# Histogram of the destinations moved into the first layer, attention terms in two parts, and the scatter ahead of the attention's gathers

## What is computed

```python
x = x + segment_sum(layernorm(x)[src] * w[:, None], dst) @ W.T + b      # 200,000 edges, dst sorted
y = layernorm(x)                                                       # layer 2
h = (y @ W_gat).reshape(M, 4, 4)                                       # 4 heads x 4 experts
a_src, a_dst = (h * att_src).sum(-1), (h * att_dst).sum(-1)
e = leaky_relu(a_src[src2] + a_dst[dst2], 0.2)                         # 131,072 edges, unsorted, + self loops
alpha = softmax of e over the edges of each dst2
scores = layernorm(segment_sum(h[src2] * alpha) + b_gat) ... .mean(heads)
out = x + sum over the 2 best experts of gate * (gelu(y @ W1[e] + b1[e]) @ W2[e] + b2[e])
```

## Time and profile before

| | |
|---|---|
| median of 3 runs | 4101.27 us (4099.21 to 4102.57) |
| the profiled execution, its own time | 4099.11 us |
| span of its trace, first to last instruction | 4097.2 us |
| mean granted TensorE clock | 0.859 |
| busy: PE, DVE, ACT, POOL | 3044.6, 1891.6, 743.4, 2766.0 us |
| block B, first instruction to barrier | 109.5 to 2066.2 |
| block of attention terms | 2066.2 to 2079.2 |
| block C | 2079.2 to 3536.3 |

### The profile page before, as it was taken

How to read it: one execution, slowest core, us unless ns; L and a number is a source line. 1 busy time by engine, 2 the same in 40 slices (tenths; PEclk the granted TensorE clock), 3 DMA queues, 4 the chain that set the end, 5 groups by cost and what they waited for, 6 DMA issues and landing times. The chain is left out here.

```text
span 4097.2 us, 58613 instructions
## 1 busy us (share of the span) xinstructions
PE 3044.6 (74%) x13541; PEld 2398.9 (59%) x13542; DVE 1891.6 (46%) x4731; ACT 743.4 (18%) x2065; POOL 2766.0 (68%) x2845
## 2 busy tenths in 40 slices
PE   1666666777878887988879999999999500266946
PEld 0444444555656665666668888888888500154734
DVE  7633444454545565444334444343431000397749
ACT  6200000001111111222222222222222100031411
POOL 6577777777777777777657777777777777301850
PEclk6877878788888998999989999999999855587978
DMA  9433333334444444444322222222222210004839
GB/s 346 144 107 105 109 112 111 114 115 115 119 117 121 119 121 121 127 127 130 112 80 64 61 64 59 63 61 64 61 64 62 44 18 4 31 23 168 305 143 363
DMA packets 298269, 450.18 MB, mean 110 GB/s; under 512 B 61272, under 2 KB 232355, under 8 KB 297507
## 3 DMA queue, kind: packets, MB, share of 16 engines
q0 software_dynamic: 114144, 216.61, 20.8%
q1 hardware_dynamic: 84847, 138.58, 9.3%
q10 hardware_dynamic: 99156, 93.60, 6.9%
HBM read 330.48 MB, written 105.96 MB: 107 GB/s over the span
## 5 line engine op out<-in xcount | busy, mean ns | idle before, releaser
L587 POOL DMA_INDIRECT rows<-feats,src_t x1500 | 1442.9, 962 | 478.3 <-issue 444.5
L723 PE MATMUL node_sums<-rows,hot 128*128 x3904 | 1080.9, 433 | 415.0 <-SPq L577 378.6
L1202 POOL DMA_INDIRECT got<-row_dram,src_sorted x1024 | 994.2, 971 | 311.9 <-issue 311.9
L723 PEld LDWEIGHTS node_sums<-rows,hot 128*128 128x128 f32 x3904 | 802.1, 213 | 655.8 <-issue 530.9
L767 DVE TENSOR_SCALAR hot<-iota,rel,ew_t 128x128 f32<-128x128 f32 x1952 | 557.7, 362 | 64.8 <-DVE rel L763 1.5
L1292 PE MATMUL d_hidden<-d_yt,w 128*128 128x256 f32 x2496 | 567.8, 381 | 0.8 <-DVE d_yt L1392 0.8
L1303 PE MATMUL d_expert<-w,hid 128*128 128x256 f32 x2496 | 564.0, 379 | 0.0
L763 DVE TENSOR_SCALAR rel<-dst_t,step_base 128x4 f32 x488 | 127.9, 262 | 925.9 <-PE node_sums L723 871.3
L1303 PEld LDWEIGHTS d_expert<-w,hid 128*128 128x128 f32 x2496 | 474.3, 190 | 64.4
L1292 PEld LDWEIGHTS d_hidden<-d_yt,w 128*128 128x128 f32 x2496 | 469.7, 191 | 62.2 <-DVE d_yt L1392 1.2
L1377 DVE TENSOR_TENSOR yo<-d_expert,b2r 128x512 f32<-128x512 f32 x156 | 107.8, 691 | 703.9 <-PE d_expert L1303 703.9
(11 more groups left out here) (304 smaller groups left out, 2972.6 us busy)
## 6 DMA issues: line engine op xcount, KB each, us to landing
ys<-y_dram SPq DMA_DIRECT2D x49, 1024.0 KB, 9.9
y_dram<-yo ACTq DMA_DIRECT2D x156, 256.0 KB, 2.3
rows<-feats,src_t POOLq DMA_INDIRECT x1500, 2.8
got<-row_dram,src_sorted POOLq DMA_INDIRECT x1024, 2.4
x_dram<-x ACTq DMA_DIRECT2D x98, 128.0 KB
xs<-x_dram SPq DMA_DIRECT2D x49, 256.0 KB, 10.8
x_ring<-in_x ACTq DMA_DIRECT2D x97, 128.0 KB
states<-got SPq DMA_DIRECT2D x64, 192.0 KB, 2.2
```

Of the source, the lines that this page charges most:

```text
L587: pool.indirect_dma_start(rows[:, g % RING, j, :], None, feats, bass.IndirectOffsetOnAxis(ap=m.src_t[:, g * GT + j:g * GT + j + 1], axis=0 ...
L723: t = pe.matmul(psA[:, ds(((code >> 1) & 1) * 512, FEAT)], hot[:, r, j, :], rows[:, ds((code >> 2) & (RING - 1), 1), j, :], start=False, s ...
L1202: pool.indirect_dma_start(got[:, k, j, 0:ROWF], None, m.row_dram, bass.IndirectOffsetOnAxis(ap=m.src_sorted[:, n * GB + j:n * GB + j + 1], ...
```

## The change

- The histogram moves from block C to block B. The 33 units of 3 or 4 quads are now one loop; after each of the first 16 VectorE makes four pieces of 16 columns (4 strips of low bits, 4 of high bits each; 512 strips in all, as before) in two buffers, and every strip waits for the strip ahead (`c.done`). TensorE counts each piece (1024 matmuls, as before). `positions` stands behind unit 16.
- The block of attention terms is gone. Its work stands at the end of block B in two parts: tiles 0 to 87 right after VectorE's last one-hots, and the last 10 tiles after the last stage. SP stores each part.
- `adst_first` is filled with zeros by SP in block B, ahead of the first `s_ready`; the loads of `att` stand ahead of the expert weights, and TensorE's first wait includes them.
- `spread` reads positions and terms in place, without copies: 22 tiles at the end of block B, 76 at the start of block C, ahead of the 1024 gathers. GpSimd waits for all of them at the end of block C.

```diff
-HCOLS = 32
+HCOLS = 16
+TERMS = [0, 88, TILES]
+SPREAD_BEFORE = 22
+def spread(pool, m, t):
+    pool.indirect_dma_start(m.adst_first, bass.IndirectOffsetOnAxis(ap=m.first_pos[:, t:t + 1], axis=0),
+                            m.node_dst[:, t, :], None, bounds_check=GEDGES - 1, oob_is_err=False
+                            ).then_inc(m.s_sc, 16)
...
@@ weighted_sums, sync
+            for n, a in enumerate((att_src, att_dst)):
+                sp.dma_start(att[:, n, :], a.rearrange("(o h) e -> o (h e)", o=1).to_broadcast([P, HE])
+                             ).then_inc(s_w, 16)
...
+            sp.wait_ge(s_pc, PC)
+            flat = m.adst_first.rearrange("(q p n) c -> q p (n c)", q=8, p=P)
+            for q in range(8):
+                sp.dma_start(flat[q], zeros[:]).then_inc(s_zo, 16)
             for g in range(RING):
                 sp.wait_ge(m.s_gn, g + 1)
                 sp.sem_inc(s_ready, 1)
...
+            sp.wait_ge(s_zo, 16 * 8)
+            for q in range(len(TERMS) - 1):
+                for n, (d, t) in enumerate(((m.row_dram, m.node_row), (m.adst_dram, m.node_dst))):
+                    sp.wait_ge(s_row, 2 * q + n + 1)
+                    sp.dma_start(d.rearrange("(p t) c -> p t c", p=P)[:, TERMS[q]:TERMS[q + 1], :],
+                                 t[:, TERMS[q]:TERMS[q + 1], :]).then_inc(s_fin, 16)
...
@@ weighted_sums, gpsimd
             for g in range(RING, GROUPS):
                 refill(g)
+            pool.wait_ge(s_pos, 1)
+            pool.wait_ge(s_zo, 16 * 8)
+            pool.wait_ge(s_row, 2)
+            for t in range(SPREAD_BEFORE):
+                spread(pool, m, t)
...
@@ weighted_sums, tensor
+            def count(q):
+                pe.wait_ge(s_hh, q + 1)
+                for j in range(HCOLS):
+                    t = pe.matmul(psC[:, 0:TILES], hot_lo[:, q % 2, j, :], hot_hi[:, q % 2, j, :],
+                                  start=False, stop=False)
+                t.then_inc(s_hm, 1)
...
@@ weighted_sums, vector
+            def hots(q):
+                if q >= 2:
+                    v.wait_ge(s_hm, q - 1)
+                for part, wide, t in ((lo, P, hot_lo), (hi, TILES, hot_hi)):
+                    for a in range(0, HCOLS, STRIP):
+                        c.done(v.tensor_tensor(t[:, q % 2, a:a + STRIP, :],
+                                               iota_b[:, None, 0:wide].to_broadcast([P, STRIP, wide]),
+                                               part[:, q * HCOLS + a:q * HCOLS + a + STRIP][:, :, None].to_broadcast(
+                                                   [P, STRIP, wide]), ALU.is_equal))
+                v.sem_inc(s_hh, 1)
...
+            for n in range(UNITS):
                 with v.Fori(CUT[n], CUT[n + 1]) as u:
                     for r in range(XS):
                         one_hots(u * XS + r, r)
+                if n < COUNTED:
+                    for q in range(PER):
+                        hots(n * PER + q)
+                if n == COUNTED:
+                    positions()
+                if n < PIECES:
+                    buf = sort_piece(n, buf)
+                if n == PIECES - 1:
+                    sort_end(buf)
+            for q in range(len(TERMS) - 1):
+                terms(q)
...
@@ gather_and_experts, gpsimd
+            for t in range(SPREAD_BEFORE, TILES):
+                spread(pool, m, t)
+            pool.wait_ge(s_pc, 1)
...
-            for k in range(2):
-                spread(0, k, first=True)
-            with pool.Fori(1, CHUNKS // 2) as i:
-                for k in range(2):
-                    spread(i, k)
-            for k in range(2):
-                pool.wait_ge(s_sc[k], 16 * CH * (CHUNKS // 2))
+            pool.wait_ge(m.s_sc, 16 * TILES)
```

More of the change, by code:

```diff
@@ L550, in weighted_sums @@
                     cur = 1 if cur == 2 else 1 - cur
+        PC = 13
         @block.sync
@@ L601, in _ @@
                             allow_small_or_imprecise_dtypes=True))
+            c.inc(pool.iota(iota_b[:], pattern=[[1, P]], base=0, channel_multiplier=0,
+                            allow_small_or_imprecise_dtypes=True))
+            c.inc(pool.memset(before[:], 1.0))
+            c.inc(pool.memset(zeros[:], 0.0))
             pool.wait_ge(s_pc, c.n)
@@ L682, in _ @@
         def _(pe):
[L684 removed]
+            pe.wait_ge(s_w, 16 * 5)
             for k in range(HALVES):
@@ L744, in _ @@
                     t.then_inc(s_turned, 1)
[L746 to L750, removed]
+                if n == PIECES - 1:
+                    pe.wait_ge(s_turn, PIECES - 9)
+                    pe.matmul(psT[:, 0:2], shift_dn[:], lastd[:], start=True, stop=True).then_inc(s_turned, 1)
             open_or_close(TILES & 1, False)
@@ L873, in _ @@
             buf = 2
-            for n in range(PIECES):
+            for n in range(UNITS):
                 with v.Fori(CUT[n], CUT[n + 1]) as u:
@@ L877, in _ @@
                         one_hots(u * XS + r, r)
[L878 to L937, removed]
-                v.sem_inc(s_row, 1)
@@ L1324, in pair @@
                         layer2(i * EXPERTS - 1, EXPERTS - 1)
-            def count(q):
-                pe.wait_ge(s_hh, q + 1)
-                for j in range(HCOLS):
-                    t = pe.matmul(psC[:, 0:TILES], hot_lo[:, j, :], hot_hi[:, j, :], start=False, stop=False)
-                t.then_inc(s_hm, 1)
             turn(0)
             pair(0, 0, first=True)
-            with pe.Fori(0, HLOOP) as u:
-                for k in range(2):
-                    count(u * 2 + k)
-                    pair(u * 2 + (k + 1), (k + 1) % 2)
-            pe.matmul(psC[:, 0:TILES], zero_b[:], zero_b[:, 0:TILES], start=False, stop=True).then_inc(s_hm, 1)
-            pe.wait_ge(s_cnt, 1)
-            pe.matmul(psC[:, P:P + TILES], m.ones[:], cnt[:], start=True, stop=True)
-            pe.matmul(psC[:, 2 * P:2 * P + TILES], before[:], cnt[:], start=True, stop=True).then_inc(s_hm, 1)
-            with pe.Fori(HLOOP, (EARLY_PAIRS - 1) // 2 - 1) as u:
+            with pe.Fori(0, (EARLY_PAIRS - 1) // 2 - 1) as u:
                 for k in range(2):
@@ L1351, in _ @@
         def _(v):
-            c = Count(v, s_v)
-            v.wait_ge(s_ei, 16)
-            c.done(v.tensor_scalar(di[:, 1, :], di[:, 0, :], P - 1, None, ALU.bitwise_and))
-            c.done(v.tensor_copy(lo[:], di[:, 1, :]))
-            c.done(v.tensor_scalar(di[:, 1, :], di[:, 0, :], 7, None, ALU.arith_shift_right))
-            c.done(v.tensor_copy(hi[:], di[:, 1, :]))
-            v.wait_ge(s_pc, 5)
-            def hots(q, n):
-                part, wide, t = ((lo, P, hot_lo), (hi, TILES, hot_hi))[n]
-                if n == 0 and not (isinstance(q, int) and q == 0):
-                    v.wait_ge(s_hm, q)
-                for a in range(0, HCOLS, STRIP):
-                    o = v.tensor_tensor(t[:, a:a + STRIP, :], iota_b[:, None, 0:wide].to_broadcast([P, STRIP, wide]),
-                                        part[:, ds(q * HCOLS + a, STRIP)][:, :, None].to_broadcast([P, STRIP, wide]),
-                                        ALU.is_equal)
-                if n == 1:
-                    o.then_inc(s_hh, 1)
             def outs(n, e, i, first=False):
@@ L1392, in out_of_psum, with pair @@
                 v.tensor_copy(yt[:, k, :, :], psY[:]).then_inc(s_yt, 1)
-            def pair(i, k, first=False, between=None, count=False):
+            def pair(i, k, first=False):
                 more = not (isinstance(i, int) and i == EARLY_PAIRS - 1)
@@ L1398, in pair @@
                 for e in range(EXPERTS):
-                    if e == 3 and between:
-                        between()
                     outs(i * EXPERTS + e, e, i, first=first)
```

170 lines of the change are left out of this document (93 added, 77 removed).

## The result

The changed kernel takes 4058.95 us (median of 4 runs, 4057.44 to 4059.93), the kernel before 4100.24 in the same comparison (4098.79 to 4102.57). The ratio is 0.9897 with an interval of 0.9882 to 0.9911: 41 us or 1.0% faster, 2 us from the forecast of 4061.

The account below looks back on a forecast made before the run. GpSimd's queue was taken as one chain through blocks B and C. Terms +5.9 +26 +94.3 -26 -140.3 = -40.1 on the profiled 4099.1 give 4059.0; with the median 2.2 above, 4061 us, range 4036 to 4092.

Parts of the forecast that it names:

- The start: Start of block B: two `att` loads and eight stores of zeros delay GpSimd's first refill by 5.9 us.
- The strips: Block B: histogram strips beside GpSimd's gathers lengthen them by 26 us in all, bounds 0 to 61.
- the sort's 0.08 a gather: Gathers beside the waited sort take 1.02, 0.08 more; over 266 gathers beside strips that makes 21 us.
- a sign of being wrong: Block B: gathers beside strips over 1.1, or refills waiting for TensorE near unit 16, would show the forecast wrong.
- The rival of the lock in full: Block B: every strip holds the port lock against GpSimd, 333 us instead of 26, 4368; chance 0.04.
- The rival that the waits let GpSimd in for nothing: Block B: waits leave gaps enough, so strips cost nothing, 4035; chance 0.09.
- The ring: Block B to unit 16: TensorE's lag costs nothing, 51 us spare; rival: it fills, 4104; with dearer strips 0.14.
- The boundary: Between blocks B and C: 22 scatters, GpSimd's DRAIN and 76 scatters make block C's gathers begin 94.3 us later.
- The tail: End of block C: only DRAIN and barrier, 8.5 instead of 148.8 us from last gather to block D, 140.3 saved.
- The end of the program: From block D on: the old length, a change of 0.
- Nothing gained: Scatters sit in GpSimd's queue anywhere; only 22, 28.4 us, find a gap, the rest is copies, barrier, wait; no chance given.
- gathers: Block C: its 1024 gathers get 26 us shorter once the histogram strips no longer stand beside them.

Follow-up runs that it names:

- moving the stores: Changed kernel with SP's eight stores of zeros behind the first 16 ready counts instead of ahead of them: 4051.66 us, ratio 0.9878.
- the PSUM row: Changed kernel with the strips' row of column numbers, now f32, read from PSUM instead of SBUF for 40 of 64 pieces: 4040.93 us, ratio 0.985.
- the 4100 setting: Comparisons in which the kernel before the change, run beside the edits of the changed kernel, took about 4100 us (4101.18 in the first).
- the 5940 setting: Two later comparisons in which the kernel before the change, run beside edits of the changed kernel, took 5935 and 5940 us.
- the run with both edits of the strips: Changed kernel with the counting row in PSUM and no waits between strips in the same 40 pieces: 6220.03 us against 5935.07, ratio 1.0481.
- the repeat of both gaining edits: Second run of the changed kernel with counting row in PSUM for 40 pieces and zero stores behind the ready counts: 4037.24 us, ratio 0.9839.

## Why the prediction was right

**The start** was forecast at +5.9 and is +6.8; the runs above put it at 5.7 to 6.8, and moving the stores gave most of it back.

**The strips** were forecast at 26. They cost 27, shown by leaving them out. The size is in part luck: 26 was block C's own loss, the sort's 0.08 a gather gave 21, and a gather wholly beside the strips took 1.10 on average, 0.15 more than alone. 90 of the 189 took over 1.1, which the prediction had named as a sign of being wrong. That the waits matter was argued ("wait as the sort does") and I did not hold to it: in the experiment without waits my own theory was the opposite, and that kernel lost 41 us. The rival of the lock in full names a thing that exists, the 14 long gathers of that run. In block B the waits between the strips kept it away; in block C before the change it was absent without waits.

**The rival that the waits let GpSimd in for nothing** is wrong: 27 us are not nothing, and of the edits tried only the PSUM row takes them away.

**The ring** costs nothing, as argued: 12.7 us of waits beyond the first against 12.2. Between 138 and 1229 us, where the forecast had 51 us to spare, TensorE still waited 78.7 for landed groups.

**The boundary** was forecast at +94.3 and is +92.4. The first scatter began 6.9 us behind the last gather's end, forecast 6.5. GpSimd's DRAIN ended 6.8 behind the last scatter instead of 8.2, and is, as said, later than SP, which waits for the last ten tiles' terms and came at 2106.1. My estimate from these rows: with 18 scatters ahead instead of 22 the DRAIN would end 5.1 us earlier, level with SP, and four scatters of 1.28 more would follow, an even exchange. Other numbers were not run in the 4100 setting.

**The tail** was forecast at -140.3 and is -143.3: the DRAIN ends 5.4 behind the last gather where I had 8.2 from the earlier trace rows. That price was too high at both barriers, by 1.4 and 2.8, and made the forecast too slow at both.

**The end of the program** is 2.1 longer, which the forecast had at nothing. From block D on the code is the same in all versions, and in the six traces of the changed kernel and its edits in the 4100 setting this part takes 560.8 to 564.7 us, against 560.9 before. So the 2.1 lie within what runs differ by, and no cause is needed.

**"Nothing gained"** held in part, as the sum had it: 98 scatters are in GpSimd's queue before and after. The boundary and the tail together give 50.9 us. Of these about 28 are the 22 scatters in a gap. About 14 are the copies: before, 139.2 us passed from the last gather's end to the last scatter's, and 98 times 1.28 are 125.4. About 4 are the wait and DRAIN behind the last indirect transfer (9.7 before, 5.5 now), and 5 the shorter rest of the gap between the blocks (46.6 before, 41.8 now).

**The total** is nearer than its parts. Start, block B and the end were longer than forecast by 0.9, 3.8 and 2.1; boundary, gathers and tail were better by 1.9, 1.4 and 3.0. The errors cancel to 0.5, and that is luck.

## What to carry to other kernels

Where one engine's queue is the chain, write the whole program as that queue's gaps and lengths; here five differences of rows were each right to within 4 us. If VectorE works beside an engine that issues indirect transfers, look at the length of those transfers; an input in PSUM took the whole cost away here, and waits between the instructions that looked superfluous kept it at 27 us instead of 71. Put no store ahead of the count that starts a pipeline. Measure in more than one setting before a result is called a gain.

## What the hardware showed that was not expected

In block B, trains of VectorE instructions with two SBUF inputs and no waits held single gathers for up to 5.25 us; with a wait between them a gather took at most 1.67; with one input in PSUM it took what it takes alone. In block C before the change trains without waits left every gather under 1.28.

In the 5940 setting TensorE crawls as long as GpSimd issues indirect transfers. Windows of the repeat without scatters ahead of the barrier (us, then PE, PEld, DVE, ACT and POOL busy with counts, granted clock, DMA share, GB/s), during block C's gathers and after them:

```profile
3230.00:4600.00 1370.00, 281.54 (x487) 138.00 (x486) 15.36 (x27) 24.35 (x58) 1033.80 (x984) 0.50 0.13 20
4700.00:5500.00 800.00, 800.00 (x3764) 704.37 (x3763) 114.23 (x200) 191.43 (x456) 0.00 (x0) 1.00 0.14 47
```

That is one matmul in 2.8 us and, with GpSimd still, one in 0.21. In the 4100 setting the changed kernel has 4634 matmuls in 985 us beside the same gathers (2215 to 3200 us). The granted clock of 0.50 (1.2 GHz) goes with the idle time and doesn't explain it, since a matmul takes 0.58 of the 2.8. With all scatters behind the gathers, TensorE stayed slow through the scatters too: in that kernel's windows 36 matmuls in 100 us beside them, 473 once they were done.

```profile
4500.00:4600.00 100.00, 20.16 (x36) 9.92 (x36) 1.39 (x3) 1.68 (x4) 75.18 (x73) 0.50 0.04 6
4700.00:4800.00 100.00, 100.00 (x473) 88.05 (x472) 14.05 (x25) 24.30 (x58) 0.00 (x0) 1.00 0.15 50
```

All versions of the changed kernel were 4.8 to 5.5% slower than the kernel before in that setting. A reason that fits is that the change puts 1024 matmuls beside block B's refills, where TensorE is then what GpSimd waits for (827 us in the run with both edits of the strips). It was not tried: the change itself and the kernel before have no trace there.

Nor is it shown that the chip makes the setting. The record numbers the chips: 12 for the first comparison (4101), 6 for the second (5935), 6 again for the repeat of both gaining edits, some five minutes later (4103), and 14 for the last (5940). The number 6 stands beside both levels, so the cause may be the chip, the machine around it, or something that passes. It is open.
